# Experts: GpSimd gathers the rows of the expert two ahead first, then makes the low part of the next gate weights

## The chip, the cores and the metric
The kernel runs on one core of one Trainium2 chip. The number is the device time of one execution in microseconds (us), as the median of three runs. The core has five engines with a queue each: PE (TensorE, matmuls), DVE (VectorE), ACT (ScalarE), POOL (GpSimd) and SP (SyncE, here only for DMAs). They run on their own and meet at semaphores.

## The reference
The input x is [8, 512, 512]; it is layer-normalised, and then goes through an RWKV block and a mixture of experts, and both results are added to x. The part in which the change stands is that of the 32 experts:

```
buf = rows of x, 256 slots for each of 32 experts      # [32, 256, 512]
g = einsum('ech,ehf->ecf', buf, w_gate)                # w_gate [32, 512, 352]
u = einsum('ech,ehf->ecf', buf, w_up)
y = einsum('ecf,efh->ech', silu(g) * u, w_down)        # w_down [32, 352, 512]
```

All is float32. Which rows go to which expert is computed in the kernel (softmax, top 4).

## The kernel before
There are three stages, one behind the other: projections and routing (`project_stage`, to about 442 us of the trace), the experts (`expert_stage`, about 442 to 877 us), and the output with the shared expert (`output_stage`). The order of every engine is written out by hand; the engines' functions are called for one expert after another by `experts`, with a hardware loop over 28 of the 32.

A float32 product is made of two parts in each operand, a high one (a rounded copy, float32r) and a low one (the value less its high part); PE multiplies three of the four pairs. So each operand passes a copy on ACT and a subtraction on DVE or POOL. In one expert e:

- SP loads the weights of expert e + 2, and stores the result rows of e.
- PE: `up_gate` for three pieces of the hidden width (72 matmuls on L1296), `turn` (L1288) transposes the gathered rows of e + 1, `down` (18 matmuls on L1323). `up_gate` of e waits for the low rows (`x_lo`) and the low gate weights (`wg_lo`) of e. `down` waits for each hidden piece's low part (`h_lo`).
- ACT: `gate_hi` for e + 1 (L1132), `silu` of piece 0 (L1154), `up_hi` for e + 1 (L1136), the high parts of the hidden pieces (L1160) with the other silus between, `rows_hi` for e + 1 (L1148), `down_hi` (L1140, L1142), `keep_y` (L1167).
- DVE: `make_index` for e + 2 (L1207), `hidden` of piece 0 (L1237), `up_lo` for e + 1 (L1216), then `hidden_lo` (L1242) and `hidden` (L1237) in turn for the three pieces, `rows_lo` for e + 1 (L1231), `down_lo` (L1222, L1224).
- POOL: `gate_lo` for e + 1 (L1108), one subtraction of 128 x 1408 elements, which waits for ACT's `gate_hi` (L1132); then `gather` for e + 2 (L1101), two indirect DMAs that fetch 128 rows each by the index that DVE's L1207 wrote. The last two experts have no gather, and the last has no L1108 either.

L1207 waits until the gather that used the same half of the index two experts earlier has landed. L1101 waits for it and for `turned`, which says that PE has read the rows that the gather overwrites:

```python
        def gather(e, half):
            wait(pool, turned, e - 1)
            wait_apart(pool, (table_loaded, 16), index_made, e + 1)
```

Of the kernel before, what the change touches and what calls it, by code (L numbers as in the profile page):

```python
# [46 lines left out]
def wait(eng, sem, value):  # L47

    if not (isinstance(value, int) and value <= 0):
        eng.wait_ge(sem, value)  # L50


def wait_apart(eng, met, sem, value):


    if not isinstance(value, int):
        value = eng.to_reg(value)
    eng.wait_ge(*met)
    wait(eng, sem, value)
# [937 lines left out]
def expert_stage(nc, bank, keep, d, shared):  # L997
# [42 lines left out]
    def experts(eng, one_expert):  # L1040


        one_expert(0, 0, 2, 1)
        with eng.Fori(0, E // 2 - 2) as r:
            one_expert(r * 2 + 1, 1, 2, r + 1)
            one_expert(r * 2 + 2, 0, 2, r + 2)
        one_expert(E - 3, 1, 2, E // 2 - 1)
        one_expert(E - 2, 0, 1, E // 2)
        one_expert(E - 1, 1, 0, E // 2)
# [46 lines left out]
    def gpsimd(pool):  # L1096
# [3 lines that stand above are left out]
            for c in range(NCT):  # L1100
                pool.indirect_dma_start(  # L1101
                    rows[half][:, c, :], None, d["z_rows"],
                    bass.IndirectOffsetOnAxis(ap=index[:, half, c, :], axis=0),
                ).then_inc(gathered[half], 16)

        def gate_lo(e, half):
            pool.wait_ge(wg_hi, e + 1)
            pool.tensor_tensor(wg[half][:, 1, :], g_in[half][:], wg[half][:, 0, :].bitcast(F32),  # L1108
                               ALU.subtract).then_inc(wg_lo, 1)

        def one_expert(e, half, more, uses):
            if more:
                gate_lo(e + 1, 1 - half)
            if more == 2:
                gather(e + 2, half)
            if not more:
                output_early[0]()

        def main(early):
            output_early.append(early)  # L1120
            gather(0, 0)
            gather(1, 1)
            experts(pool, one_expert)

        output_early = []
        return main
# [1059 lines left out]
```

## Time and profile before

| | |
|---|---|
| median of 3 runs | 1708.35 us (1705.87 to 1712.76) |
| profiled execution | 1710.3 us, span 1708.3 us |
| PE busy | 1652.7 us, 97% of the span |
| DVE busy | 1257.2 us, 74% |
| POOL busy | 846.4 us, 50% |
| ACT busy | 690.1 us, 40% |
| chain that ended last | PE 82%, DVE 7%, issue 5%, POOL 3%, DMA 2% |

The span is what the trace covers; times in it count from its start. "Busy" leaves out waits, with one exception: an instruction that has started and then stands because something else holds what it needs counts as busy to its end. The mean length of such a group is then longer than the work. In the timelines a row is one instruction, or several of one kind (x4); the brackets at its end say how long the engine was idle before it and what ended that.

### The profile page before, as it was taken

The page shows a single profiled execution, that of the slowest core. Times are in us where ns is not written, and L with a number is a line of the kernel's source. Part 1 is how long each engine was busy: PE and PEld are TensorE (multiplying, and loading weights), DVE is VectorE, ACT ScalarE, POOL GpSimd, SP SyncE. Part 2 cuts the span into 40 slices and gives each one's busy share as a digit, 9 for nine tenths or more (in the row PEclk, how much of TensorE's full clock was granted, in tenths as well). Part 3 has the DMA queues.
Part 4 walks back from the last instruction along what each step waited for, and adds up shares of the span by engine and source line. Part 5 has one row for each costly group of instructions (what it writes and reads, how often), then busy time and mean ns, then how long its engine had stood idle before and what let it go on. Part 6 is the DMA issues. An engine that isn't in the chain of part 4 may idle for free.

```text
span 1708.3 us, 26221 instructions
## 1 busy us (share of the span) xinstructions
PE 1652.7 (97%) x8496; PEld 1403.2 (82%) x8496; DVE 1257.2 (74%) x1848; ACT 690.1 (40%) x1213; POOL 846.4 (50%) x707
## 2 busy tenths in 40 slices
PE   5989999999999999999998999999999999999998
PEld 4777877877899999999986788888888888888887
DVE  6988998887555555555557877776877768687776
ACT  4656565654566666666653212121221212112120
POOL 3678777776444444444446544352443525243351
PEclk8999999999999999999999999999999999999999
DMA  4443434324666666666686655454545343433431
GB/s 154 184 162 137 161 144 151 141 106 175 240 233 239 242 243 241 232 226 226 240 275 216 196 199 183 170 180 151 179 137 181 101 157 118 154 105 123 159 101 44
DMA packets 122938, 299.17 MB, mean 175 GB/s; under 512 B 20508, under 2 KB 31772, under 8 KB 118240
## 3 DMA queue, kind: packets, MB, share of 16 engines
q1 hardware_dynamic: 103104, 263.82, 43.6%
q0 software_dynamic: 19456, 33.67, 7.0%
q8 instruction: 50, 0.82, 0.2%
q10 hardware_dynamic: 288, 0.52, 0.1%
q14 instruction: 40, 0.33, 0.1%
HBM read 233.34 MB, written 81.36 MB: 184 GB/s over the span
## 4 chain that ended last, share of the span: by engine, by line
PE 82%; DVE 7%; issue 5%; POOL 3%; DMA 2%; ACT 1%; DVEq 0%; another core or an unknown queue 0%; SPq 0%; POOLq 0%; ACTq 0%
PE bank L1983 24%; PE bank L1296 16%; PE bank L934 13%; PE bank L1997 12%; PE bank L1323 8%; PE bank L2014 5%; PE bank L1288 2%; POOL slot_tokens L368 1%; PE bank L893 1%; PE bank L876 1%; DVE mixf L686 1%; DVE s_total L1835 1%; DMA wr_staged<-in_Wr 0%; POOL mix L354 0%; DVE s_ek L1818 0%
## 5 line engine op out<-in xcount | busy, mean ns | idle before, releaser
L934 PE MATMUL bank<-mix,w 128*128 128x512 f32 x1536 | 371.7, 399 | 14.0 <-DVE mix L693 5.2
L934 PEld LDWEIGHTS bank<-mix,w 128*128 128x128 f32 x1536 | 289.6, 191 | 83.6 <-issue 9.3
L1983 PE MATMUL bank<-s_zT,s_wg 128*128 128x512 f32 x1056 | 257.1, 393 | 7.0 <-ACT s_act_g L1672 3.7
L1983 PE MATMUL bank<-s_zT,s_wu 128*128 128x512 f32 x1056 | 254.4, 390 | 7.2 <-DVE bank L1779 7.2
L1997 PE MATMUL bank<-s_wd,s_h 128*128 128x512 f32 x1056 | 253.8, 389 | 0.4 <-DVE s_h L1785 0.4
L1983 PEld LDWEIGHTS bank<-s_zT,s_wg 128*128 128x128 f32 x1056 | 200.0, 190 | 50.5 <-issue 8.8
L1983 PEld LDWEIGHTS bank<-s_zT,s_wu 128*128 128x128 f32 x1056 | 197.7, 188 | 50.6 <-issue 9.8
L1997 PEld LDWEIGHTS bank<-s_wd,s_h 128*128 128x128 f32 x1056 | 198.2, 188 | 41.8 <-issue 0.8
L1108 POOL TENSOR_TENSOR e_wg<-e_g_in,e_wg 128x1408 fp32r<-128x1408 f32 x31 | 101.1, 3263 | 208.7 <-ACT e_wg L1132 208.7
L1579 POOL DMA_INDIRECT s_picked<-y_rows,s_slot x128 | 140.2, 1096 | 83.9 <-DVE s_total L1835 44.9
L1672 ACT ACTIVATE s_act_g<-bank 128x512 f32<-128x512 f32 x88 | 52.5, 596 | 286.2 <-PE bank L1983 279.0
L368 POOL DMA_INDIRECT slot_tokens<-token,slot x128 | 138.7, 1084 | 51.2 <-issue 29.8
L1296 PE MATMUL bank<-e_xT,e_wg 128*128 128x256 f32 (+1 forms) x1152 | 152.2, 282 | 1.2 <-DVE e_xT L1231 1.2
L1683 ACT ACTIVATE s_h<-bank 128x512 fp32r<-128x512 f32 x80 | 47.9, 599 | 258.9 <-DVE bank L1779 255.9
L1296 PE MATMUL bank<-e_xT,e_wu 128*128 128x256 f32 (+1 forms) x1152 | 152.1, 282 | 0.0
L1296 PEld LDWEIGHTS bank<-e_xT,e_wg 128*128 128x128 f32 (+1 forms) x1152 | 144.3, 180 | 4.2 <-DVE e_xT L1231 1.7
L1296 PEld LDWEIGHTS bank<-e_xT,e_wu 128*128 128x128 f32 (+1 forms) x1152 | 142.1, 180 | 0.0
L354 POOL TENSOR_TENSOR mix<-mixf,mix 128x512 fp32r<-128x512 f32 x88 | 118.7, 1359 | 46.5 <-ACT mix L471 45.4
L1323 PE MATMUL bank<-e_wd,e_h 128*128 128x512 f32 (+1 forms) x576 | 140.1, 396 | 0.0
L1835 DVE SCALAR_TENSOR_TENSOR s_total<-s_picked,s_rec,s_total 128x512 f32<-128x512 f32 x128 | 136.3, 1065 | 3.7 <-DVE s_total L1835 0.5
L1323 PEld LDWEIGHTS bank<-e_wd,e_h 128*128 128x128 f32 (+1 forms) x576 | 106.2, 189 | 21.4
L1599 POOL TENSOR_TENSOR s_att<-s_gate,s_att 128x512 fp32r<-128x512 f32 x32 | 45.6, 1425 | 156.6 <-ACT s_att L1701 156.6
(165 smaller groups left out, 2434.0 us busy)
## 6 DMA issues: line engine op xcount, KB each, us to landing
s_wu<-wu_split SPq DMA_DIRECT2D x77, 512.0 KB
e_g_in<-in_w_gate SPq DMA_DIRECT2D x32, 704.0 KB
e_u_in<-in_w_up SPq DMA_DIRECT2D x32, 704.0 KB
e_d_in<-in_w_down SPq DMA_DIRECT2D x32, 512.0 KB
y_rows<-e_y SPq DMA_DIRECT2D x32, 512.0 KB, 2.9
s_zT<-zT_parts SPq DMA_DIRECT2D x16, 1024.0 KB, 7.1
zT_parts<-zT_hi SPq DMA_DIRECT2D x8, 1024.0 KB
zT_parts<-zT_lo SPq DMA_DIRECT2D x8, 1024.0 KB
```

Of the source, the lines that this page charges most:

```text
L354: pool.tensor_tensor(mix[:, i % 2, k, 1, :], mixf[:, k, :], mix[:, i % 2, k, 0, :].bitcast(F32), ALU.subtract).then_inc(lo_made, 1)
L368: pool.indirect_dma_start(d["slots"], bass.IndirectOffsetOnAxis(ap=slot[:, half, at:at + 1], axis=0), token[:, half, at // TOPK:at // TOPK ...
L934: last = pe.matmul(pj[m][:], w[i][:, w_part, k, m * P:(m + 1) * P], mix[:, i % 2, k, x_part, :], start=(k == 0 and q == 0), stop=(k == KC ...
L1108: pool.tensor_tensor(wg[half][:, 1, :], g_in[half][:], wg[half][:, 0, :].bitcast(F32), ALU.subtract).then_inc(wg_lo, 1)
L1296: last = pe.matmul(gu[f][0:m, which, :], w[half][:, w_part, k * F + f0:k * F + f0 + m], xT[half][:, x_part, k, :], start=(q == 0 and k == ...
L1323: last = pe.matmul(yp[c][:], h[0:m, f, h_part, c * P:(c + 1) * P], wd[half][0:m, w_part, f, :], start=(f == 0 and q == 0), stop=(f == NF - ...
L1579: pool.indirect_dma_start(picked[:, k, :], None, d["y_flat"], bass.IndirectOffsetOnAxis(ap=slot[:, j * TOPK + k:j * TOPK + k + 1], axis=0) ...
L1672: act.activation(act_g[:, i, :], gp[:], ACT.Silu).then_inc(silu_made, 1)
L1835: dve.scalar_tensor_tensor(total[:, j, :], picked[:, k, :], rec[:, at:at + 1], total[:, j, :], ALU.mult, ALU.add).then_inc(picked_used, 1)
L1983: last = pe.matmul(into[:], w[:, w_part, k, :], zT[:, x_part, k, :], start=(q == 0 and k == 0), stop=(q == 2 and k == KC - 1))
L1997: last = pe.matmul(yp[j][:], h[:, i, h_part, j * P:(j + 1) * P], wd[f][:, w_part, :], start=(f == 0 and q == 0), stop=(f == NFS - 1 and q ...
L2014: last = pe.matmul(ob[j % 2][:], att[m][:, x_part, j * P:(j + 1) * P], wo[m][:, w_part, :], start=(m == 0 and q == 0), stop=(m == KC - 1 a ...
```

## The change
On POOL, in each expert, the call of `gather` for e + 2 is placed ahead of the call of `gate_lo` for e + 1. All else stays.

```diff
         def one_expert(e, half, more, uses):
+            if more == 2:
+                gather(e + 2, half)
             if more:
                 gate_lo(e + 1, 1 - half)
-            if more == 2:
-                gather(e + 2, half)
             if not more:
                 output_early[0]()
```

POOL's queue before, from the first gathers through the first expert and the loop over two experts, to its end. L1101 is the pair of gathers into one of the two row buffers, L1108 the low part of the gate weights:

```order
L1101 DMA e_rows_120<-z_rows,keep_index 128x512 x2
L1108 TENSOR_TENSOR e_wg_108<-e_g_in_114,e_wg_108 128x1408
L1101 DMA e_rows_119<-z_rows,keep_index 128x512 x2
L1044 UNCONDITIONAL_BRANCH
L1044 ISA
L1108 TENSOR_TENSOR e_wg_107<-e_g_in_113,e_wg_107 128x1408
L50 REGISTER_ALU
L57 REGISTER_ALU
L1101 DMA e_rows_120<-z_rows,keep_index 128x512 x2
L1108 TENSOR_TENSOR e_wg_108<-e_g_in_114,e_wg_108 128x1408
```

The same place now:

```order
L1101 DMA e_rows_120<-z_rows,keep_index 128x512 x2
L1101 DMA e_rows_119<-z_rows,keep_index 128x512 x2
L1108 TENSOR_TENSOR e_wg_108<-e_g_in_114,e_wg_108 128x1408
L1044 UNCONDITIONAL_BRANCH
L1044 ISA
L57 REGISTER_ALU
L1101 DMA e_rows_120<-z_rows,keep_index 128x512 x2
L1107 REGISTER_ALU
L1108 TENSOR_TENSOR e_wg_107<-e_g_in_113,e_wg_107 128x1408
L57 REGISTER_ALU
```

In the first expert and in each of the loop the pair of gathers has moved from behind the subtraction to ahead of it. The queues of the other engines are the same row by row. At the loop's end the last expert with a gather has the same order, and the last L1108 stands alone:

```order
L1101 DMA e_rows_120<-z_rows,keep_index 128x512 x2
L1108 TENSOR_TENSOR e_wg_107<-e_g_in_113,e_wg_107 128x1408
L1108 TENSOR_TENSOR e_wg_108<-e_g_in_114,e_wg_108 128x1408
```

Before, the first of these three rows stood between the other two.

## Rows read from the trace of the kernel before

**Rows 1.** Windows: stretch, length, busy us of each engine, TensorE's clock, DMA share, GB/s.

```profile
455.50:864.10 408.60, 408.60 (x2942) 386.01 (x2940) 241.27 (x420) 267.07 (x481) 187.56 (x88) 1.00 0.67 238
...
876.80:1700.00 823.20, 808.62 (x3542) 665.80 (x3541) 620.84 (x679) 164.84 (x272) 342.93 (x307) 1.00 0.47 152
```

**Rows 2.** Waits from 441.8 to 864: who waited for whom, total us, times, longest.

```profile
POOL e_wg L1108 <- ACT e_wg L1132: 208.7, 31, 7.0
```

**Rows 3.** Timeline of PE: start us, length us, engine, line, operation, output<-inputs, shape.

```profile
605.32 1.59 PE L1296 MATMUL bank<-e_xT,e_wg 128*128 128x256 f32 x12
...
614.72 4.38 PE L1323 MATMUL bank<-e_wd,e_h 128*128 128x512 f32 x18
618.94 1.59 PE L1296 MATMUL bank<-e_xT,e_wg 128*128 128x256 f32 x12
```

**Rows 4.** Timeline of POOL in the same experts.

```profile
607.46 3.24 POOL L1108 TENSOR_TENSOR e_wg<-e_g_in,e_wg 128x1408 fp32r<-128x1408 f32 x1 [6.80 <-ACT e_wg L1132]
610.85 2.16 POOL L1101 DMA_INDIRECT e_rows<-z_rows,keep_index  x1
613.32 0.96 POOL L1101 DMA_INDIRECT e_rows<-z_rows,keep_index  x1 [0.31 <-issue]
621.08 3.23 POOL L1108 TENSOR_TENSOR e_wg<-e_g_in,e_wg 128x1408 fp32r<-128x1408 f32 x1 [6.81 <-ACT e_wg L1132]
```

**Rows 5.** Timeline of ACT.

```profile
608.64 1.37 ACT L1136 ACTIVATE e_wu<-e_u_in 128x1408 fp32r<-128x1408 f32 x1
...
617.61 0.63 ACT L1142 ACTIVATE e_wd<-e_d_in 96x512 fp32r<-96x512 f32 x1
...
619.63 1.37 ACT L1132 ACTIVATE e_wg<-e_g_in 128x1408 fp32r<-128x1408 f32 x1
```

**Rows 6.** Timeline of DVE.

```profile
610.05 2.14 DVE L1216 TENSOR_TENSOR e_wu<-e_u_in,e_wu 128x1408 fp32r<-128x1408 f32 x1 [0.85 <-ACT e_wu L1136]
612.11 0.41 DVE L1242 TENSOR_TENSOR e_h<-e_act_g,e_h 128x256 fp32r<-128x256 f32 x1
...
616.08 1.66 DVE L1231 SCALAR_TENSOR_TENSOR e_xT<-bank,keep_const,e_xT 128x256 fp32r<-128x256 f32 x4 [0.30 <-ACT e_xT L1148]
...
619.41 0.68 DVE L1224 TENSOR_TENSOR e_wd<-e_d_in,e_wd 96x512 fp32r<-96x512 f32 x1
620.02 0.16 DVE L1207 COPY keep_index<-keep_table 128x2 uint32 x1
...
623.75 2.05 DVE L1216 TENSOR_TENSOR e_wu<-e_u_in,e_wu 128x1408 fp32r<-128x1408 f32 x1 [0.85 <-ACT e_wu L1136]
```

**Rows 7.** Timeline of POOL in the first expert.

```profile
443.11 4.04 POOL L1108 TENSOR_TENSOR e_wg<-e_g_in,e_wg 128x1408 fp32r<-128x1408 f32 x1 [5.41 <-ACT e_wg L1132]
448.57 1.89 POOL L1101 DMA_INDIRECT e_rows<-z_rows,keep_index  x1 [1.42 <-DVE keep_index L1207]
```

**Rows 8.** Timeline of DVE in the first expert.

```profile
442.83 1.22 DVE L1222 TENSOR_TENSOR e_wd<-e_d_in,e_wd 128x1024 fp32r<-128x1024 f32 x1
443.96 3.73 DVE L1224 TENSOR_TENSOR e_wd<-e_d_in,e_wd 96x512 fp32r<-96x512 f32 x1
447.62 0.15 DVE L1207 COPY keep_index<-keep_table 128x2 uint32<-128x2 uint32 x1
...
448.02 1.61 DVE L1216 TENSOR_TENSOR e_wu<-e_u_in,e_wu 128x1408 fp32r<-128x1408 f32 x1
449.56 0.41 DVE L1242 TENSOR_TENSOR e_h<-e_act_g,e_h 128x256 fp32r<-128x256 f32 x1
...
450.78 0.45 DVE L1242 TENSOR_TENSOR e_h<-e_act_g,e_h 128x256 fp32r<-128x256 f32 x1 [0.48 <-ACT e_h L1160]
...
452.76 1.66 DVE L1231 SCALAR_TENSOR_TENSOR e_xT<-bank,keep_const,e_xT 128x256 fp32r<-128x256 f32 x4 [0.30 <-ACT e_xT L1148]
```

**Rows 9.** Timeline of DVE and POOL in the output stage.

```profile
941.80 3.55 DVE L1874 TENSOR_TENSOR s_wg<-s_piece,s_wg 128x512 fp32r<-128x512 f32 x1
...
943.51 1.28 POOL L1616 TENSOR_TENSOR s_wu<-s_piece,s_wu 128x512 fp32r<-128x512 f32 x1
```

## The prediction
> **What bounds the kernel now.** I read the share of each engine first and found the experts' stretch: TensorE is busy for all of it, 408.60 us of 408.60 us between 455.5 and 864.1 us, at a granted clock of 1.00 (the 2.4 GHz level), while POOL is busy for 188 us of it [rows 1]. In the waits of that stretch POOL's wait for ScalarE ahead of L1108 is the longest by far, 208.7 us in 31 waits [rows 2]; it costs nothing, since no row shows PE behind it. So the change can hardly gain there, and the question is whether it makes PE wait. The timelines of one expert answer that. PE begins two experts 13.62 us apart (605.32 and 618.94), and its down product begins at 614.72 [rows 3]. Below, times in an expert count from PE's first gate matmul, 605.32: the down product is at +9.40, the next expert at +13.62.
>
> Two things must be there in time for PE: the first low hidden part (`hidden_lo`, L1242) by +9.40, and the low part of the next rows (`rows_lo`, L1231) by +13.62. The latter ends at 617.74, that is +12.42 [rows 6], so DVE's chain has 1.20 us to spare in an expert, and no more.
>
> **What holds DVE and POOL apart now.** POOL's L1108 runs from 607.46 to 610.70 (+2.14 to +5.38) [rows 4], nearly all of it in the time in which DVE waits for the first silu. DVE's L1216 (two inputs in SBUF, 1408 elements) is let go by ScalarE's L1136 at 610.01 [rows 5], starts at 610.05 and takes 2.14 us to 612.19 [rows 6], though the same instruction took 1.61 us at 448.02 [rows 8]. Its end is 1.49 us behind the end of L1108. In the next expert L1108 ends at 624.31 [rows 4] and L1216 at 625.80 [rows 6]: again 1.49. So L1216 stands still until L1108 is through, and then needs 1.49 us. The other way about: L1108 at 443.11 was due while L1222 ran (until 444.05), took 4.04 instead of 3.24 us and ended at 447.15 [rows 7]; L1224, next on DVE and already due at 443.96, took 3.73 us instead of the 0.68 of 619.41 and ended at 447.69, 0.54 behind it [rows 6, 8]. So whichever runs is let through, and a waiting L1108 gets in ahead of DVE's next instruction. The output stage shows the same: L1874, with 512 elements as L1224, was due at 941.80, let POOL's L1616 start ahead of it at 943.51, and ended at 945.35, 0.56 us behind that one's 944.79 [rows 9].
>
> **The change, part by part.** Nothing is added or removed. In 30 experts (0 to 29) POOL's two gathers (L1101) go ahead of its one L1108; PE, ACT, DVE and SP keep their order. Before, L1108 waited for ScalarE's L1132, and the gathers came behind it. Now the gathers need the index (L1207) of DVE, the first of DVE in an expert, done at 620.18, which is +1.24 [rows 6]. A gather begins 0.80 us behind the index: 447.77 to 448.57 [rows 7, 8]. A gather that nothing holds takes 0.95 us, with 0.30 us ahead of the second [rows 4]. Two thus end 0.80 + 0.95 + 0.30 + 0.95 = 3.00 us behind the index, and L1108 starts some 0.03 later, at index + 3.03.
>
> What is queued behind that is L1108 alone; its own result (wg_lo) is wanted by PE only at the next expert's start and by SP's load later still, so its lateness as such is covered: even at +10 it leaves over 3 us. The rows that are gathered earlier are wanted by `turn` one expert later, so that is no gain. The gathers move the same bytes a few us earlier; the DMA share is 0.67 in the stretch [rows 1], so a third of 13.62 us, 4.5 us an expert, is unused, and that covers what two gathers push aside; I cost it at 0, from both sides, since gathers that come before the weights only change places with them.
>
> The cost is that L1108 moves from DVE's idle time into DVE's working time. Worked out for a steady state, in which `rows_lo` sets PE's start, so that it ended at -0.04 (0.04 us is what passes from ScalarE's end at 610.01 to DVE's start at 610.05 [rows 5, 6]):
> - The index ends 2.44 us behind `rows_lo` (617.74 to 620.18 [rows 6]): +2.40. ScalarE's L1142 ends 0.50 behind it (618.24) and L1132 at most 2.76 behind L1142 (621.00), hence by +3.22 [rows 5]; L1136 started at +3.32 before (608.64), with one short silu ahead of it, so it is 0.2 us late at most. I take L1216 as due at +4.73, as before.
> - The gathers: +3.20 to +5.40. The second starts at +4.45, ahead of L1216. L1108 is due at +5.43.
> - L1216 runs +4.73 to +6.34 (1.61). L1108 waits, gets in at +6.34 and ends at +9.58 (3.24).
> - L1242 of the first part, before at 612.52 (+7.20), ends about 0.3 behind L1108: +9.87. PE's down product starts at +9.91 instead of +9.40: 0.51 us of waiting.
> - From there the chain of hidden, high part, low part and rows runs tight. The first expert shows this length, since DVE was late there as well: L1242 ended at 449.97 and L1231 at 454.42, 4.45 us later [rows 8]. So `rows_lo` ends at +14.32 and PE starts the next expert at +14.36 instead of +13.62. The down product, which ends at 13.62 + 0.51 = +14.13, is no longer what it waits for.
> Per expert that is 0.74 us. And the state reproduces itself, since `rows_lo` ends 0.04 us ahead of PE's start again. The first expert gets there at once: without L1108 ahead, L1224 takes 0.68, ends at 444.64, the index at 444.73, the gathers at 447.73; L1108 then waits for L1216. The last two experts have no gather, and return to the order of before. Sum: 30 x 0.74 = 22.2 us.
>
> What the price could be: from below nothing (rival 2). From above, if L1242 takes its usual 0.41 us behind L1108 and each of the hops of ScalarE costs 0.04 more, 14.5, which is 0.9 an expert and 27 us. Against the profiled execution (1710.3 us, span 1708.3) the sum is 1732.5 us; against the median of 1708.35 us it is 1730.6 us, and the forecast is 1731 us. The shift isn't taken back: behind the experts PE is busy for 808.62 of 823.20 us [rows 1].
>
> **Rivals.**
> 1. *The gathers are slower than I take them, and the second starts behind L1216.* In the trace a gather that starts behind L1216 stands until that ends: 610.85 to 613.01, 2.16 instead of 0.95 us, its end 0.82 behind L1216's 612.19 [rows 4, 6]. The second gather, due at +4.45, need be only 0.28 us later for that. Then it ends at 6.34 + 0.82 = +7.16, the first L1242 comes through at +6.67, L1108 runs +7.19 to +10.43 and holds up the second L1242 (due 0.81 us behind the first, by 449.97 and 450.78, so at +7.48) until +10.73. From the second L1242 to the end of L1231 the first expert has 451.23 to 454.42, 3.19 us [rows 8]: +13.92 and PE at +13.96. That is 0.34 an expert, 10 us: 1719. For it speaks that 0.80 comes from two places only; against it that both had the same value. The SBUF — State Buffer page of the Trainium skill (Who interferes with whom) says that tensor_tensor takes only the read side of the shared port and so does not stall the making of descriptors on GpSimd. By that rule this rival would not exist, and the sum would stay at 22 us for a late gather too; the row of 2.16 us speaks against the rule here.
> 2. *Not slower: DVE's first L1242 gets in ahead of the waiting L1108.* Then L1242 ends at +6.67, L1108 runs to +9.91, the second L1242 ends at about +10.24 and `rows_lo` at 10.24 + 3.19 = +13.43, ahead of +13.58. PE waits for nothing and the time stays at 1708. The turning point is whether `rows_lo` is through by +13.58. For it: it is one arbitration, at an instant where both are ready. Against: at 443.96 and at 941.80 DVE lost just this.
> 3. *The long L1216 has another cause than L1108.* Then moving L1108 does nothing to DVE: 1708, or a few tenths less as L1224 at 443.96 loses its 3.05 us, which PE did not wait for. Two ends at exactly 1.49 us speak against it.
> 4. *Worse than computed:* PE's two waits an expert (0.51 and 0.23 us) take the clock to its lower level, or POOL holds DVE twice. In the stretch behind the experts PE idles 14.58 us in 823 and keeps 1.00, so I give it little; over 1740.
>
> **How the numbers follow.** Forecast (0.7 to 0.9 us an expert) 62%, rival 1 17%, rivals 2 and 3 together 14%, rival 4 5%, a small gain from something not seen 2%. A measurement of this kernel tells about 0.5% (8.5 us) from no change. Of rival 1 most lies above 1716.9. Faster 0.03, same 0.14, slower 0.83. The range is 1714 to 1740: the forecast's own spread (1724 to 1738) and rival 1, with rivals 2 to 4 left out.
>
> **What would show it.** In the profile of the changed kernel: PE's gate matmuls 14.3 to 14.5 us apart in the experts and a wait of PE for L1231 and for L1242 in every expert; gathers of 0.95 us both; L1108 at about 4.2 us on average, starting near +5.4; L1216 at 1.6 us; the first L1242 at 3 us and more. L1216 at 1.6 and L1242 at 0.41 with PE unbroken would make rival 2 right; a second gather of 2 us or more, rival 1. If L1216 stays at 2.1 us, the chain from the index is wrong.

## The result
The changed kernel takes 1746.81 us (median of 4 runs, 1746.4 to 1750.58), the kernel before 1708.39 us beside it (1705.87 to 1712.76). The ratio is 1.0229, with a 95% interval of 1.0216 to 1.0241: 38.4 us slower, outside the range that was given. The direction was right, the size was not: 22.2 us were forecast.

The profile of the changed kernel has a span of 1748.6 us. First the windows of the two stretches that answer to [rows 1] (length, busy us of PE, PEld, DVE, ACT and POOL, clock, DMA share, GB/s):

```profile
453.00:900.00 447.00, 424.42 (x2941) 386.06 (x2942) 329.16 (x420) 258.91 (x482) 152.47 (x88) 1.00 0.59 217
900.00:1748.60 848.60, 824.83 (x3643) 679.74 (x3641) 634.87 (x703) 171.49 (x287) 345.29 (x314) 1.00 0.48 154
```

From the second expert's first gate matmul to that of the last expert the kernel before took 408.6 us (455.50 to 864.10), this one 446.9 (453.01 to 899.90): 38.3 us more. The 29 experts of this stretch that have the move (1 to 29) are 14.94 us apart on average, 1.32 us more each, nearly all by turns 14.86 and 15.02; expert 30, which has no gather, takes 13.72. The first expert, ahead of the stretch, takes 14.25 us (438.76 to 453.01) instead of 13.72. PE is idle for 22.6 us of the first window, where it had no gap (447.00 less 424.42); the other 15.8 us stand in the record as busy (424.42 against 408.60 for the same matmuls), since the ends of matmuls are modelled. Its clock stays at 1.00. Then the waits of the experts, which answer to [rows 2]:

```profile
POOL e_rows L1101 <- DVE keep_index L1207: 279.6, 30, 9.5
PEld bank L1323 <- DVE e_h L1242: 25.8, 29, 1.0
PE bank L1323 <- DVE e_h L1242: 21.0, 29, 0.9
PEld bank L1296 <- issue: 7.6, 14, 0.7
PEld bank L1296 <- DVE e_xT L1231: 6.8, 16, 0.5
```

POOL no longer waits for ScalarE but for DVE's index, and PE waits for both of the instructions that the prediction named: for L1242 in 29 experts, and ahead of the next expert 30 times, 16 of them put down to L1231 and 14 to no releaser ("issue"; PEld is PE's weight load). The timelines of one expert, which answer to [rows 3, 4, 6], show the size (columns as there). The timeline of PE:

```profile
612.83 4.44 PE L1323 MATMUL bank<-e_wd,e_h 128*128 128x512 f32 x18 [0.69 <-DVE e_h L1242]
...
617.27 1.69 PE L1296 MATMUL bank<-e_xT,e_wg 128*128 128x256 f32 x12
...
627.78 4.40 PE L1323 MATMUL bank<-e_wd,e_h 128*128 128x512 f32 x18 [0.76 <-DVE e_h L1242]
...
632.30 1.68 PE L1296 MATMUL bank<-e_xT,e_wg 128*128 128x256 f32 x12
```

The timeline of POOL over the same two experts:

```profile
606.74 0.95 POOL L1101 DMA_INDIRECT e_rows<-z_rows,keep_index  x1 [0.30 <-issue]
607.72 3.24 POOL L1108 TENSOR_TENSOR e_wg<-e_g_in,e_wg 128x1408 fp32r<-128x1408 f32 x1
620.42 0.96 POOL L1101 DMA_INDIRECT e_rows<-z_rows,keep_index  x1 [9.47 <-DVE keep_index L1207]
...
622.66 3.24 POOL L1108 TENSOR_TENSOR e_wg<-e_g_in,e_wg 128x1408 fp32r<-128x1408 f32 x1
```

And that of DVE:

```profile
607.31 5.13 DVE L1216 TENSOR_TENSOR e_wu<-e_u_in,e_wu 128x1408 fp32r<-128x1408 f32 x1 [0.85 <-ACT e_wu L1136]
612.37 0.41 DVE L1242 TENSOR_TENSOR e_h<-e_act_g,e_h 128x256 fp32r<-128x256 f32 x1
...
615.55 1.66 DVE L1231 SCALAR_TENSOR_TENSOR e_xT<-bank,keep_const,e_xT 128x256 fp32r<-128x256 f32 x4 [0.30 <-ACT e_xT L1148]
...
619.49 0.16 DVE L1207 COPY keep_index<-keep_table 128x2 uint32 x1
...
622.10 5.29 DVE L1216 TENSOR_TENSOR e_wu<-e_u_in,e_wu 128x1408 fp32r<-128x1408 f32 x1 [0.85 <-ACT e_wu L1136]
627.32 0.41 DVE L1242 TENSOR_TENSOR e_h<-e_act_g,e_h 128x256 fp32r<-128x256 f32 x1
...
630.50 1.66 DVE L1231 SCALAR_TENSOR_TENSOR e_xT<-bank,keep_const,e_xT 128x256 fp32r<-128x256 f32 x4 [0.30 <-ACT e_xT L1148]
```

Look at L1216. It is due at 607.31, inside the second gather (606.74 to 607.69) and 0.41 us before L1108 starts, and it takes 5.13 us: it ends 1.48 us behind the end of L1108 (610.96). In the next expert it starts 0.56 us ahead of L1108 and takes 5.29, again 1.49 behind L1108's end at 625.90. In all of the experts 1 to 29 it is 0.38 to 0.57 us ahead of L1108 and takes 5.12 to 5.30 us. The forecast had it run first, in 1.61 us.

So the experts hang in a ring that leaves out PE. From L1231's end at 617.21: 2.44 us to the end of the index (619.65), 0.77 to the gather (620.42), 5.48 to the end of L1108 (625.90), 1.49 to the end of L1216 (627.39), 0.34 to the end of L1242 (627.73), 4.43 to the end of the next L1231 (632.16). The sum is 14.95 us, which is the mean distance of the 29 experts within 0.02, and PE, whose own work in an expert is 13.62 us, follows at 617.27 and 632.30.

### The profile page after: what moved, and what is told of

It reads as the page before. It is cut to its first block, busy times and chain, and to the rows that moved or that the text cites. A ratio compares the mean times of both kernels' runs of the same rounds, so it can differ in the third digit from the quotient of the medians.

```text
span 1748.6 us, 26221 instructions
## 1 busy us (share of the span) xinstructions
PE 1668.3 (95%) x8496; PEld 1401.9 (80%) x8496; DVE 1344.7 (77%) x1848; ACT 681.5 (39%) x1213; POOL 809.8 (46%) x707
## 4 chain that ended last, share of the span: by engine, by line
PE 67%; issue 13%; DVE 10%; ACT 4%; POOL 4%; DMA 2%; SPq 0%; DVEq 0%; POOLq 0%; ACTq 0%
PE bank L1983 24%; PE bank L1997 12%; PE bank L934 11%; PE bank L1323 8%; PE bank L1296 6%; PE bank L2014 5%; ACT e_wu L1136 2%; POOL slot_tokens L368 1%; DVE e_wu L1216 1%; DVE mixf L686 1%; DVE e_h L1242 1%; PE bank L893 1%; POOL mix L354 1%; PE bank L876 1%; DVE s_total L1835 1%
## 5 line engine op out<-in xcount | busy, mean ns | idle before, releaser
L1101 POOL DMA_INDIRECT e_rows<-z_rows,keep_index x64 | 62.6, 978 | 293.7 <-DVE keep_index L1207 283.6
L1216 DVE TENSOR_TENSOR e_wu<-e_u_in,e_wu 128x1408 fp32r<-128x1408 f32 x32 | 157.0, 4905 | 27.4 <-ACT e_wu L1136 27.4
```

Source lines behind the costliest of these rows:

```text
L1101: pool.indirect_dma_start(rows[half][:, c, :], None, d["z_rows"], bass.IndirectOffsetOnAxis(ap=index[:, half, c, :], axis=0),).then_inc(ga ...
L1216: dve.tensor_tensor(wu[half][:, 1, :], u_in[half][:], wu[half][:, 0, :].bitcast(F32), ALU.subtract).then_inc(wu_lo, 1)
```

## The experiments
Two accounts stood against each other. In the first, POOL's subtraction L1108 stands where DVE needs what both share, and holds up the chain that feeds PE; the gathers only push it there. In the second, gathers ahead of L1108 cost in themselves, by their descriptors or their transfers. Line numbers differ by two less to eight more in kernels with moved or added lines; the names are those of the tiles. The ratio of each run is to executions of the kernel before taken beside it, with medians of 1709.18 us (subtraction on DVE, one gather, subtraction late, subtraction behind L1216) and 1707.65 us (the other four).

### The subtraction moved to DVE

```diff
 POOL, one_expert:
             if more == 2:
                 gather(e + 2, half)
-            if more:
-                gate_lo(e + 1, 1 - half)
 DVE, one_expert:
                 make_index(e + 2, half, uses + 1)
+            if more:
+                gate_lo(e + 1, 1 - half)
             hidden(e, 0)
```

> The gathers stay first, and POOL's subtraction (L1108) is taken away from it: DVE makes the low part of the next gate weights itself, between the index and the first hidden product, where it idles. Theory (the subtraction on POOL keeps DVE's two-input instructions out, and its place in time is the whole loss): L1216 takes 1.6 us, the new DVE instruction takes 1.6 us and fits in the 3.4 us between the index and L1216, rows_lo ends near +12 and PE starts an expert every 13.62 us again: 1708 us. Rival (the early gathers themselves cost, by their descriptors or by their transfers beside the weight loads): the experts stay 14.9 us apart, 1747 us.

Measured: 1708.08 us, ratio to the kernel before 0.9988 (0.9979 to 0.9998). The gathers are as early as in the changed kernel, and the whole loss is gone. The timeline of DVE in this run:

```profile
606.16 0.16 DVE L1205 COPY keep_index<-keep_table 128x2 uint32 x1
607.11 1.64 DVE L1209 TENSOR_TENSOR e_wg<-e_g_in,e_wg 128x1408 fp32r<-128x1408 f32 x1 [0.79 <-ACT e_wg L1130]
...
609.74 1.63 DVE L1214 TENSOR_TENSOR e_wu<-e_u_in,e_wu 128x1408 fp32r<-128x1408 f32 x1 [0.65 <-ACT e_wu L1134]
```

The moved subtraction (here L1209) lies in the idle time that DVE had between the index and the first hidden product. L1216 (here L1214) is at its undisturbed 1.63 us, and PE's experts are 13.62 us apart. The second account falls. The second gather of a pair stands for L1209 a little here (1.23 us at 608.35, where L1209 ends at 608.75), and nobody in the experts waits for it.

### One gather ahead instead of two

```diff
+            if more == 2:
+                gather(e + 2, half, (0,))
             if more:
                 gate_lo(e + 1, 1 - half)
             if more == 2:
-                gather(e + 2, half)
+                gather(e + 2, half, (1,))
```

> Half of the move: of the two gathers only the first goes ahead of L1108, the second stays behind it. Theory: in the state of before, the gather runs from about +2.1 to +3.05 and L1108 from +3.1 to +6.3; L1216, due at +4.73, is held and ends at 6.3 + 1.49 = +7.8 (3.1 us long) instead of +6.87, and rows_lo ends some +12.6, still ahead of +13.56: the slack takes it all, 1708 us. Rival (each gather that is moved costs the same, or the loss is proportional to L1108's delay): half of 38 us, 1727 us.

Measured: 1712.16 us, ratio 1.0018 (1.0008 to 1.0028). The timeline of DVE in one expert, whose PE start is 606.82:

```profile
604.90 1.66 DVE L1234 SCALAR_TENSOR_TENSOR e_xT<-bank,keep_const,e_xT 128x256 fp32r<-128x256 f32 x4 [0.30 <-ACT e_xT L1151]
...
608.84 0.16 DVE L1210 COPY keep_index<-keep_table 128x2 uint32 x1
...
611.55 3.93 DVE L1219 TENSOR_TENSOR e_wu<-e_u_in,e_wu 128x1408 fp32r<-128x1408 f32 x1 [0.85 <-ACT e_wu L1139]
615.40 0.41 DVE L1245 TENSOR_TENSOR e_h<-e_act_g,e_h 128x256 fp32r<-128x256 f32 x1
...
618.59 1.66 DVE L1234 SCALAR_TENSOR_TENSOR e_xT<-bank,keep_const,e_xT 128x256 fp32r<-128x256 f32 x4 [0.30 <-ACT e_xT L1151]
```

The loss is not in proportion: 3 us and not 19. But L1231 ends at 620.25, +13.43, where I had written +12.6. I had taken the index where it stood before the change; it is itself behind L1231, so it moved as well (609.00 is +2.18, not +1.24). The ring has here 2.44 + 0.77 + 4.22 + 1.49 + 0.33 + 4.44 = 13.69 us, just about PE's own 13.62. PE goes on at 620.45, and its experts are 13.62 to 13.80 us apart; from the second to the last they take 410.2 us instead of 408.6, and the first takes 14.36 us instead of 13.72. That is most of the small loss.

### Only the subtraction late, with no gather moved

```diff
 the kernel before, POOL, gate_lo:
             pool.wait_ge(wg_hi, e + 1)
+            pool.wait_ge(h_hi, (e - 1) * NF + 1)
             pool.tensor_tensor(
```

> The order of before (L1108 first, then the gathers), but L1108 also waits for the first high hidden part (h_hi, L1160), which comes at +5.00, when L1216 has been running for 0.3 us. It makes alone, without any early gather, the state that the prediction assumed for the changed kernel: L1216 +4.73 to +6.34 at 1.6 us, L1108 waiting and then +6.34 to +9.58, the first L1242 ending at about +9.9 (3 us and more in the trace), PE 0.75 to 0.9 us late in each of 31 experts. Theory: 1731 to 1736 us, with gathers behind L1108. If DVE's L1242 gets in ahead of the waiting L1108: 1708 us. Rival (the gathers cost, not L1108): 1708 us as well, but with L1242 at 0.41 us and L1108 undisturbed.

Measured: 1733.57 us, ratio 1.0136 (1.0119 to 1.0153). It is the arrangement of the forecast, and it costs what the forecast said: from the second expert to the last 431.2 us instead of 408.6, 0.75 us an expert. The timeline of POOL in this run has L1108 (here L1109):

```profile
604.00 4.36 POOL L1109 TENSOR_TENSOR e_wg<-e_g_in,e_wg 128x1408 fp32r<-128x1408 f32 x1 [7.76 <-ACT e_h L1161]
...
618.30 4.35 POOL L1109 TENSOR_TENSOR e_wg<-e_g_in,e_wg 128x1408 fp32r<-128x1408 f32 x1 [7.57 <-ACT e_h L1161]
```

And that of DVE at the same place:

```profile
603.65 1.63 DVE L1217 TENSOR_TENSOR e_wu<-e_u_in,e_wu 128x1408 fp32r<-128x1408 f32 x1 [0.84 <-ACT e_wu L1137]
605.19 3.45 DVE L1243 TENSOR_TENSOR e_h<-e_act_g,e_h 128x256 fp32r<-128x256 f32 x1
...
611.41 1.66 DVE L1232 SCALAR_TENSOR_TENSOR e_xT<-bank,keep_const,e_xT 128x256 fp32r<-128x256 f32 x4 [0.30 <-ACT e_xT L1149]
```

L1216 (here L1217) started 0.35 us ahead of L1108 (0.35 to 0.42 in all experts), ran in 1.63 us and made it wait (4.36 us instead of 3.24); L1108, waiting, then got in ahead of DVE's next instruction, which took 3.45 us instead of 0.41. PE's first gate matmuls lie 14.3 to 14.4 us apart; the prediction had 14.36.

### The subtraction less late

```diff
 the kernel before, POOL, gate_lo:
             pool.wait_ge(wg_hi, e + 1)
+            pool.wait_ge(h_made, (e - 1) * NF + 1)
             pool.tensor_tensor(
```

> The order of before, but L1108 also waits for the first hidden product (h_made, L1237), which comes at +3.88: L1108 runs from +3.96 to +7.20, 1.8 us later than before and 1 us earlier than in the run with the wait for L1160. Theory: L1216, due at +4.73, is held and ends at +8.68 (3.9 us long), the first L1242 at +9.0 (PE wants it by +9.40), rows_lo at +13.45 (PE wants it by +13.58): DVE looks 1.8 us busier in each expert and the time stays at 1708 to 1711 us. Rival (every microsecond that DVE is held costs its share): between 1708 and 1734 us in proportion, about 1723 us.

Measured: 1711.26 us, ratio 1.0020 (1.0010 to 1.0029). The timeline of DVE in this run:

```profile
609.43 3.95 DVE L1217 TENSOR_TENSOR e_wu<-e_u_in,e_wu 128x1408 fp32r<-128x1408 f32 x1 [0.85 <-ACT e_wu L1137]
...
616.51 1.66 DVE L1232 SCALAR_TENSOR_TENSOR e_xT<-bank,keep_const,e_xT 128x256 fp32r<-128x256 f32 x4 [0.30 <-ACT e_xT L1149]
```

L1216 (L1217) is held for 2.3 us in every expert, and L1231 ends at 618.17, +13.55 from PE's start at 604.62. PE goes on at 618.32, 0.08 us later than it would have. So 2.3 us of standing still cost under 0.1 us an expert (411.1 us instead of 408.6 from the second to the last). In the run above DVE stands for 3.0 us (3.45 instead of 0.41), 0.7 more, and PE's experts are 0.7 us further apart.

### The subtraction behind L1216

```diff
 the changed kernel, POOL, gate_lo:
             pool.wait_ge(wg_hi, e + 1)
+            pool.wait_ge(wu_lo, e + 1)
             pool.tensor_tensor(
```

> The changed kernel, and POOL's L1108 also waits until DVE's L1216 is done (wu_lo). Theory: L1216 runs unhindered (1.6 us, to about +6.4), L1108 then holds up either the first L1242 (if it gets in ahead of it; PE starts an expert 0.75 to 0.9 us late, 1731 to 1735 us) or only the second (if DVE's next instruction is in first, which is likelier here, since POOL hears of the end of L1216 only behind it: rows_lo ends by +13.5, 1708 us). Rival (the gathers cost): 1747 us or more, since L1108 is later still.

Measured: 1710.51 us, ratio 1.0009 (1.0000 to 1.0019). With gathers first and L1108 later still than in the changed kernel, nearly all of the loss is gone. The timeline of DVE in this run, with PE's start at 605.55:

```profile
610.27 1.63 DVE L1217 TENSOR_TENSOR e_wu<-e_u_in,e_wu 128x1408 fp32r<-128x1408 f32 x1 [0.84 <-ACT e_wu L1137]
611.82 0.42 DVE L1243 TENSOR_TENSOR e_h<-e_act_g,e_h 128x256 fp32r<-128x256 f32 x1
...
613.05 2.54 DVE L1243 TENSOR_TENSOR e_h<-e_act_g,e_h 128x256 fp32r<-128x256 f32 x1 [0.48 <-ACT e_h L1161]
...
617.13 1.66 DVE L1232 SCALAR_TENSOR_TENSOR e_xT<-bank,keep_const,e_xT 128x256 fp32r<-128x256 f32 x4 [0.30 <-ACT e_xT L1149]
```

L1216 and the first L1242 pass; the second is held (2.54 us), and L1231 still ends at 618.79, +13.24. This is the price of the prediction's rival 2, about nothing, but here a semaphore decided it.

### A gap between the gathers and the subtraction

```diff
 the changed kernel, POOL, one_expert:
                 gather(e + 2, half)
+                pool.memset(spare[:], 0.0).then_inc(gap, 1)
+                pool.wait_ge(gap, e + 1)
             if more:
                 gate_lo(e + 1, 1 - half)
```

> The changed kernel with one more instruction on POOL: behind the second gather a memset of 120 columns of a tile that nobody reads, and L1108 waits for it, so that L1108 no longer stands ready right behind a gather. It starts some 0.3 us later for that. Theory (a POOL instruction that stands ready behind a gather shuts DVE's two-input instructions out about half a us ahead of its own start in the trace, so that L1216, which starts 0.4 to 0.6 us ahead of it and inside the gather, stands still): here L1216 starts inside the second gather again, but gets through in 1.6 us; L1108 waits for it and takes 4 us and more, the first L1242 takes the wait (3 us and more), and PE starts an expert every 14.4 to 14.5 us as with the late subtraction: 1732 to 1736 us, faster than the changed kernel although L1108 stands later. Rival (the gather itself keeps DVE out to its own end): L1216 about 2.1 us, L1108 behind it, 1745 us or more. Rival (L1216 is simply too late for L1108 in any case): L1216 stays at 5.1 to 5.3 us and the time rises by 30 x 0.3 us to 1756 us.

Measured: 1733.01 us, ratio to the kernel before 1.0143 (1.0126 to 1.0160), so 13 to 14 us less than the changed kernel, by an instruction and a wait more. The timeline of POOL in this run:

```profile
614.10 0.97 POOL L1103 DMA_INDIRECT e_rows<-z_rows,keep_index  x1 [7.91 <-DVE keep_index L1211]
615.37 0.95 POOL L1103 DMA_INDIRECT e_rows<-z_rows,keep_index  x1 [0.30 <-issue]
616.32 0.21 POOL L1116 MEMSET e_spare<- 128x120 f32 x1
616.61 3.86 POOL L1110 TENSOR_TENSOR e_wg<-e_g_in,e_wg 128x1408 fp32r<-128x1408 f32 x1
```

And that of DVE:

```profile
615.78 1.63 DVE L1220 TENSOR_TENSOR e_wu<-e_u_in,e_wu 128x1408 fp32r<-128x1408 f32 x1 [0.85 <-ACT e_wu L1140]
617.32 3.43 DVE L1246 TENSOR_TENSOR e_h<-e_act_g,e_h 128x256 fp32r<-128x256 f32 x1
```

L1216 (here L1220) starts in the second gather as before, at 0.41 us behind the gather's start, and passes in 1.63 us; L1108 starts only at 616.61 and waits (3.86 us), and the first L1242 stands for 3.43 us. It is the arrangement of the forecast again, this time with the gathers in front. The gather itself does not keep L1216 out, then. L1108 also starts later here, 0.75 to 0.86 us behind L1216 and not 0.38 to 0.57, so this run alone doesn't say whether the lead or the place right behind the gather decides. Nor does the lead decide alone: in the run with the subtraction late 0.35 us were enough, where L1108 stood behind a wait for h_hi, and in the changed kernel 0.38 to 0.57 were not. So neither the gather alone nor a short lead alone makes L1216 stand, but the two together. Two readings are left: an L1108 that stands ready behind a running gather is served first, or L1216 needs a longer lead while a gather runs, somewhere between 0.57 and 0.75 us. Whether the memset or the wait lets L1216 through was not separated either, and in no run is L1108 right behind another instruction than a gather.

### Half of the subtraction

```diff
 the changed kernel, POOL, gate_lo: columns 0 to 703 only
+DVE, one_expert, behind make_index: columns 704 to 1407
```

> The changed kernel, with half of L1108: POOL makes the low part of 704 of the 1408 columns (1.62 us), DVE the other 704 (0.85 us) right behind the index, where it idles. Theory (a ring from one expert to the next sets the pace: end of rows_lo, 2.44 us to the index, 0.77 to the gather, 2.21 for two gathers, L1108, 1.49 for the rest of L1216, 0.34 for L1242, 4.43 to the end of rows_lo; 14.95 us with 3.24 us of L1108): the ring is 13.33 us, shorter than PE's own 13.62, and the whole loss goes, 1708 to 1710 us. Rival (the loss is proportional to what POOL keeps DVE out): half of it stays, 1728 us.

Measured: 1707.38 us, ratio 0.9997 (0.9987 to 1.0007). L1216 (here L1222) is held here too, 2.81 us instead of 1.63, at no cost. The timeline of POOL has the half L1108:

```profile
607.51 1.72 POOL L1109 TENSOR_TENSOR e_wg<-e_g_in,e_wg 128x704 fp32r<-128x704 f32 x1
```

That of DVE has the held L1216:

```profile
607.92 2.81 DVE L1222 TENSOR_TENSOR e_wu<-e_u_in,e_wu 128x1408 fp32r<-128x1408 f32 x1 [0.85 <-ACT e_wu L1137]
```

Half of the length took the whole loss away. That is what the ring gives (13.33 us worked out, 13.43 with the 1.72 us of this L1108, both below PE's 13.62), and not a proportion.

### The index ahead of down_lo

```diff
 the changed kernel, DVE, one_expert:
-            if more == 2:
-                make_index(e + 2, half, uses + 1)
             hidden(e, 0)
 ...
                 rows_lo(e + 1, 1 - half)
+                if more == 2 and not (isinstance(e, int) and e == E - 3):
+                    make_index(e + 3, 1 - half, uses + half + 1)
                 down_lo(e + 1, 1 - half)
```

(and the index of expert 2 in `main`, ahead of the first `down_lo`.)

> The changed kernel, with gathers first on POOL, but DVE makes the index right behind rows_lo, ahead of down_lo, and not behind down_lo. One link of the ring (rows_lo to index, 2.44 us) becomes about 0.2 us. Theory: the gathers then run from about -0.1 to +2.1 of the next expert, L1108 starts at about +2.15 when ScalarE's high part is there, as before the change, L1216 takes 2.1 us, PE starts every 13.62 us, 1708 us. Rival (gathers ahead of L1108 cost in themselves): 1747 us.

Measured: 1708.34 us, ratio 1.0012 (1.0001 to 1.0022). The time is as expected, the way is not quite. The timeline of POOL in this run:

```profile
615.13 1.73 POOL L1101 DMA_INDIRECT e_rows<-z_rows,keep_index  x1 [7.29 <-DVE keep_index L1207]
617.17 0.95 POOL L1101 DMA_INDIRECT e_rows<-z_rows,keep_index  x1 [0.30 <-issue]
618.14 3.25 POOL L1108 TENSOR_TENSOR e_wg<-e_g_in,e_wg 128x1408 fp32r<-128x1408 f32 x1
```

The first gather meets L1222 on DVE, a subtraction with both inputs in SBUF (614.81 to 616.04), stands for it and takes 1.73 us; so L1108 starts at 618.14, 2.66 us behind PE's start at 615.48 and not 2.15, and L1216 takes 2.6 us in this expert and 2.75 in the next, not 2.1. The slack covers it.

## Why the prediction was wrong in its size
- **That PE would be made to wait, by L1108 in DVE's working time: right.** With L1108 off POOL nothing is left of the loss, and with L1108 alone late the loss is there without any gather moved.
- **The gathers' place and length: right.** 0.77 us behind the index (0.80 forecast), 0.95 to 0.96 each, L1108 right behind. That they cost nothing themselves is right as well. Their landing takes 6.7 us at the median instead of 4.7, and nobody in the experts waits for it.
- **"L1216 runs +4.73 to +6.34": wrong, and this is the step that failed.** It came inside the second gather, as foreseen (+4.83 from 617.27), and I let it through because L1108's own row starts later. It stood until L1108 was through. So L1108 takes 3.24 us and not 4.2, L1216 5.1 to 5.3 and not 1.6, and the first L1242 0.41 and not 3. In the forecast its 1.6 us lay ahead of L1108; in fact 1.49 us of it lie behind. L1242 ends at +10.46 (627.73 from 617.27) and not +9.87, and that is the 0.59 us an expert that is missing: 0.74 forecast, 1.33 by the ring, 1.32 measured over experts 1 to 29. Why L1216 lost although it started first is known only so far: it did where L1108 stood ready right behind a gather, and not where a wait stood ahead of L1108. Why that is so stays open.
- **The rows of before held it.** L1874 in [rows 9] was due at 941.80, 1.71 us ahead of L1616, but inside a gather with another subtraction (L1613, at 942.26) right behind it, and it stood through both. The prediction showed the second of the two, and read it as L1874 letting that one start ahead; L1874 was 0.46 us ahead of the first, and lost to that. The same pattern asked of L1216, with the prediction's other terms as they were, gives 5.43 + 3.24 + 1.49 + 0.34 + 4.45 = +14.95 for `rows_lo` and +14.99 for PE, 1.37 us an expert and 1749 us. The timeline of POOL before at that place:

```profile
941.24 1.00 POOL L1579 DMA_INDIRECT s_picked<-y_rows,s_slot  x1 [0.30 <-issue]
942.26 1.30 POOL L1613 TENSOR_TENSOR s_wd<-s_piece,s_wd 128x512 fp32r<-128x512 f32 x1
```

- **"A waiting L1108 gets in ahead of DVE's next instruction": right**, by the late subtraction and by the gap: the first L1242 takes 3.4 us in both.
- **The tail of 4.45 us and the 2.44 us to the index: right** (4.43 and 2.44). With the arrangement that the prediction assumed, PE starts experts 14.3 to 14.4 us apart against 14.36 worked out.
- **"The state reproduces itself": right, but for another reason.** I tied L1216 to PE's start. In the changed kernel none of the ring's times is a wait for PE. That doesn't make it free of PE: L1216 is let go by ScalarE's L1136, behind the silu that reads PE's first product, and so PE still sets where in the gathers L1216 falls due. No run made PE faster.
- **Rival 1** came true in one expert, the first: the second gather started 0.05 us behind L1216 and took 2.39 us. As a forecast for all of them it was wrong. That a gather stands behind DVE's subtraction, against what the Trainium skill's page SBUF — State Buffer says in "Who interferes with whom", is seen again there and in the run with the early index (1.73 us); the page calls its reason inferred, and the rows decide. **Rival 2** did not happen of itself, and its price was right where a semaphore made it happen. **Rival 3** is excluded by the run with L1108 off POOL, in which L1216 takes 1.63 us. **Rival 4**: the clock stayed at 1.00.
- **The first expert** did not get there at once, as the prediction had it. L1224 did lose its stall, as foreseen, but L1216 passed, the second L1242 stood instead, and the expert took 0.53 us more and not 0.74.

The timeline of POOL in that first expert:

```profile
442.51 0.94 POOL L1101 DMA_INDIRECT e_rows<-z_rows,keep_index  x1 [7.76 <-DVE keep_index L1207]
443.75 2.39 POOL L1101 DMA_INDIRECT e_rows<-z_rows,keep_index  x1 [0.30 <-issue]
446.17 3.23 POOL L1108 TENSOR_TENSOR e_wg<-e_g_in,e_wg 128x1408 fp32r<-128x1408 f32 x1
```

And that of DVE, where L1216 is 0.05 us ahead of the second gather, and the second L1242 stands for L1108:

```profile
443.70 1.63 DVE L1216 TENSOR_TENSOR e_wu<-e_u_in,e_wu 128x1408 fp32r<-128x1408 f32 x1 [0.97 <-ACT e_wu L1136]
...
446.48 3.21 DVE L1242 TENSOR_TENSOR e_h<-e_act_g,e_h 128x256 fp32r<-128x256 f32 x1 [0.48 <-ACT e_h L1160]
```

What stays open: in the profiled executions the part behind the experts is 848.7 us long (899.90 to 1748.6) against 844.2 before, and the part ahead of them is 3.0 us shorter (438.76 against 441.78). In the other runs' profiles the part behind the experts is 843 to 847 us, and the part ahead of them 437.7 to 441.9. The profiled execution was also the longest of the four (1750.58 us; the others 1746.4 to 1746.91). No cause was looked for.

## What to carry to other kernels
An instruction that shares a resource with another engine has a place in time, and not only a place in its queue: before moving it, ask what it was idle beside. Here a subtraction lay for the most part in another engine's gap. Letting DVE stand for 2.3 us an expert cost 3 to 4 us in all, 3.0 us cost 24, and 3.6 us (5.2 instead of 1.6, the change) cost 38. Then follow the chain until it comes back to its start: if it closes without the bounding engine, its sum is the new pace, and shortening a link until the sum is below the bounding engine's own time brings everything back at once. Two links were tried here, half of the work and an earlier index, and both did.

## What the hardware showed that was not expected
The earlier start in the rows did not always win. L1216, with a start 0.38 to 0.57 us ahead of L1108's, lost to it when L1108 stood right behind a gather; with a memset and a wait between (and a lead of 0.75 to 0.86 us), it passed, and with L1108 behind a plain wait 0.35 us were enough. So the start of a row does not tell by itself which of two instructions gets what they share. The gather itself did not keep DVE out: in the run with the gap, L1216 started inside it and took 1.63 us. And the changed kernel with one more instruction and one more wait was 13 to 14 us faster than without.
